# One-hot of the source rows in a GNN kernel: compared with a repeated tile of node numbers instead of with one number per partition

## The reference

```python
src = edge_index[0]
dst = edge_index[1]
msg = x[src] * edge_weight[:, None]
agg = jax.ops.segment_sum(msg, dst, num_segments=x.shape[0])
h = agg + x
h = jax.nn.relu(h @ W1 + b1)
return h @ W2 + b2
```

## Time and profile before

| | us |
|---|---|
| median of 3 runs | 3583.42 |
| lowest and highest of them | 3581.49, 3587.07 |
| the profiled execution | 3582.05 |
| its span | 3580.3 |
| of it `source_rows`, from its first `select` to its last `low_part` | about 481 |

### The profile page before, as it was taken

How to read it: one execution, slowest core, us unless ns; L and a number is a source line. 1 busy time by engine, 2 the same in 40 slices (tenths; PEclk the granted TensorE clock), 3 DMA queues, 4 the chain that set the end, 5 groups by cost and what they waited for, 6 DMA issues and landing times. The chain is left out here.

```text
span 3580.3 us, 48965 instructions
## 1 busy us (share of the span) xinstructions
PE 1964.5 (55%) x14483; PEld 1255.0 (35%) x14483; DVE 2622.0 (73%) x4729; ACT 879.1 (25%) x1649; POOL 2221.9 (62%) x2224
## 2 busy tenths in 40 slices
PE   2455555555555655555555555266505666657775
PEld 2122222222222222222222222166505555557773
DVE  5477777777677677677777777366789999977775
ACT  3122222222222222222222222011224555520002
POOL 0377777777777777777777777311275555555552
PEclk7787888888878787888888777589855555569998
DMA  9533233332332332332333332379708999989991
GB/s 307 147 102 92 91 103 91 97 97 91 98 96 90 98 96 90 100 93 91 103 91 95 98 91 72 119 273 339 279 5 269 304 305 306 303 328 412 414 402 46
DMA packets 219404, 601.78 MB, mean 168 GB/s; under 512 B 96175, under 2 KB 113455, under 8 KB 206615
## 3 DMA queue, kind: packets, MB, share of 16 engines
q1 hardware_dynamic: 147914, 385.44, 33.6%
q0 software_dynamic: 67488, 210.15, 15.8%
q10 hardware_dynamic: 3861, 4.33, 0.4%
HBM read 403.92 MB, written 195.84 MB: 168 GB/s over the span
## 5 line engine op out<-in xcount | busy, mean ns | idle before, releaser
L1085 POOL DMA_INDIRECT region_rows<-x_space,pos x1664 | 1628.8, 979 | 531.4 <-issue 505.7
L943 PE MATMUL ps_cnt<-ident,rest 128*128 128x128 f32 x832 | 177.8, 353 | 804.5 <-DVE rest L1027 804.5
L871 ACT CAST x_space<-ps_cnt 128x512 bf16<-128x512 f32 x208 | 121.9, 586 | 1456.0 <-PE ps_cnt L943 1456.0
L943 PEld LDWEIGHTS ps_cnt<-ident,rest 128*128 128x128 f32 x832 | 116.9, 177 | 979.6 <-issue 979.6
L1016 DVE TENSOR_REDUCE rank<-masked 128x8 f32<-128x784 f32 x208 | 323.0, 1553 | 21.4
L996 DVE COPY x_space<-edges_space 128x16 f32 (+1 forms) x208 | 39.2, 189 | 332.4 <-DMA region_rows<-x_space,pos 331.7
L1457 POOL TENSOR_TENSOR agg<-x_space,agg 128x576 f32<-128x576 f32 x131 | 179.4, 1369 | 143.2 <-ACT agg L1437 143.2
L929 PE MATMUL ps_fx<-window,x_space 128*64 128x512 bf16 x1248 | 240.8, 506 | 0.0
L1421 PE MATMUL ps_th<-tmp_space,x_space 128*128 128x64 bf16 x2646 | 143.1, 230 | 177.6 <-DVE x_space L1385 177.6
L1032 DVE TENSOR_TENSOR ps_agg<-ps_cnt,x_space 128x512 f32<-128x512 f32 x208 | 145.5, 700 | 128.8 <-ACT x_space L871 128.8
L906 PE MATMUL ps_th<-x_space,w_wf 128*128 128x512 f32 x416 | 224.8, 624 | 9.7 <-DMA x_space<-rbf 9.7
(11 more groups left out here) (247 smaller groups left out, 4544.3 us busy)
## 6 DMA issues: line engine op xcount, KB each, us to landing
tmp_space<-region_rows SPq DMA_DIRECT2D x98, 882.0 KB, 6.6
run_rows<-agg SPq DMA_DIRECT2D x98, 873.0 KB, 4.8
x_space<-key_rows SPq DMA_DIRECT2D x98, 576.0 KB, 5.8
x_space<-rbf SPq DMA_DIRECT2D x104, 512.0 KB, 3.7
tmp_space<-rel_rows SPq DMA_DIRECT2D x104, 512.0 KB, 4.0
region_rows<-x_space,pos POOLq DMA_INDIRECT x1664, 2.3
region_rows<-x_space SPq DMA_DIRECT2D x1, 14259.0 KB, 83.6
x_space<-part_rows SPq DMA_DIRECT2D x208, 48.0 KB, 2.0
```

The lines of the kernel that those rows point to most:

```text
L943: last = e.transpose(ps_cnt[:, t * P:(t + 1) * P], product[:, t * P:(t + 1) * P], ident[:, :])
L1085: e.indirect_dma_start(out=region_rows, out_offset=bass.IndirectOffsetOnAxis(ap=pos[j][:, t:t + 1], axis=0), in_=rows_f[j][:, t, :], in_of ...
```

## The change

A tile `node_rep`, 128x128 bf16, is added; in `set_up` DVE fills each of its rows with `node_1`. In `source_rows`, `select` compares the keys with this tile, repeated over the 9 tiles of the half, by a tensor-tensor instruction; the instruction before compared them with the one number per partition by a tensor-scalar instruction. Output, order and waits are the same.

```diff
@@ -163,6 +163,7 @@
         ident_b = sb("ident_b", [P, P], BF16)
+        node_rep = sb("node_rep", [P, P], BF16)
         ones = sb("ones", [P, P], BF16)
@@ -555,6 +556,7 @@
                     step(e.tensor_scalar(node_1, node_iota[:, 0:1], 1.0, None, ALU.add))
+                    step(e.tensor_copy(node_rep[:, :], node_1.broadcast_to([P, P])))
@@ -1382,8 +1384,9 @@
                             e.wait_ge(mm, n - 1)
-                        e.tensor_scalar(which[n % 2], key_bc[b % KB][:, (n % 2) * U * P:(n % 2 + 1) * U * P], node_1, None,
-                                        ALU.is_equal).then_inc(oh, 1)
+                        by_tile = lambda a: a.rearrange("p (t q) -> p t q", q=P)
+                        e.tensor_tensor(by_tile(which[n % 2]), by_tile(key_bc[b % KB][:, (n % 2) * U * P:(n % 2 + 1) * U * P]),
+                                        node_rep[:, None, :].broadcast_to([P, U, P]), ALU.is_equal).then_inc(oh, 1)
```

## The result

| | us |
|---|---|
| before, median of 4 runs | 3583.36 |
| changed kernel, median of 4 runs | 3640.78 (3638.10 to 3642.67) |
| ratio | 1.0154, 95% interval 1.0140 to 1.0168 |
| predicted | 3638, range 3618 to 3656 |
| `source_rows`, before and after | 481.1 and 533.5 |

What follows compares the result with a forecast made beforehand. DVE was taken to bound `source_rows`, held up by exclusion with POOL's subtraction. 98 regions at +0.57 us gave 56, less about half a microsecond: +55.5 on 3582.05 gave 3637.6, taken as 3638, range 3618 to 3656.

Steps and rivals of the forecast that it cites:

- The constant: In `set_up`, one 128x128 copy added to DVE's chain: 0.15 to 0.4 us, covered by DMA, so 0.
- S alone: `select` of a region's first half, without contention: tensor-tensor 752 ns instead of 0.51 us, a term of +0.24 us.
- S excludes GpSimd: In `source_rows`, the new `select` and POOL's subtraction still do not run together, both ways; first subtraction 1.65 us long.
- S': `select` of a region's other half, held up by POOL: issued at 3.74, ends at 5.54.
- The cycle: One region of `source_rows`, `multiply` to next region's `multiply`: 4.90 us grows by 0.57 to 5.47, 98 times.
- M': `multiply` of a region's other half: at 1.79 before, predicted at 2.02 after the change.
- P': POOL's subtraction for a region's other half: asked for at 3.57, begins at 3.67, ends at 4.91.
- 0.12 hidden in S': Second `select` hides 0.12 beside POOL, as `low_part` does, ending 0.63 behind; with 0.19 the cycle grows by 0.50.
- GpSimd slips in ahead of S: Rival: POOL's subtraction goes before a region's first `select`; a region 6.66 us, +172 us, 3754; chance 0.05.
- S' ahead of P': Rival: second `select` gets the ports before POOL's second subtraction; 3573 to 3583; chance 0.04 below 0.2%, 0.03 within.
- the order at 1.53 and at 3.67: In a region, first `select` precedes POOL's subtraction asked at 1.53; POOL's second precedes second `select` at 3.67.

Runs made afterwards that it cites:

- the two orders: Subtraction always under `multiply`, with `low_part` last or waiting for `select`, each in kernel before and changed kernel: ratios 1.0042 and 1.0138; 1.0006 and 1.0137.

## Why the prediction was right

- **DVE sets the stage.** It stayed busy 531.93 of 533.50 us; PE's matmuls took 1.62 us and covered nothing up.
- **The constant** cost 0.23 us in the set-up. DVE's chain ends at 73.1 there and the next stage's first work begins at 111.7, so the stores still cover it, and the kernel with the tile alone is at 1.0005.
- **S alone, +0.24.** 742 to 754 ns measured, 752 worked out from two bf16 comparisons of other lengths. The formula of the Trainium skill, page "VectorE: DVE Perf Modes", gives 756 as an estimate and is as near; it erred on the instruction that was taken out (456 against 516), and the sum by it, 12 us more, would have been worse.
- **S excludes GpSimd.** Yes, in both directions, as the rows from two other stages said: the subtraction asked for at 1.53 lasts 1.65 us for 1.24, and S' 1.80 for 0.74. The kernel with the numbers in PSUM shows the case without.
- **The cycle, +0.57.** 5.44 - 4.90 = 0.54. No step of the table above is off by more than 0.04 (M' comes at 2.00, P' is issued 1.53 after it instead of 1.55). The choice of 0.12 hidden in S', and not 0.19, was right: S' ends 0.62 behind P'. 98 x 0.54 = 53 us against 55.5 forecast and 52.4 measured for the stage.
- **The time.** That 3638 was within 3 us of 3640.8 is in part luck: the stage came out 3 us short of the forecast, and some 5 us outside it, which no term foresaw, made up for that. Between the two profiled executions 7.3 us lie outside the stage, 3.5 of them in `region_sums` and the rest mostly in `run_sums`, and this is scatter, as the kernel with the tile alone shows.
- **The rivals.** That GpSimd slips in ahead of S, or S' ahead of P', did not happen in the regular regions; the order at 1.53 and at 3.67 held with 0.20 and 0.19 us.

The same working missed afterwards, in the expectations for the two orders: the step that failed was "0.08 to begin", which I had taken from the distance between ACT's cast and GpSimd's start. From DVE's end to GpSimd's start it is 0.17, and a subtraction that already stands in line begins 0.14 before that end, so 0.31 us of each half went unused. And DMA waits belong in the sum as soon as a cycle is to fall under 4.9: the share of 0.90 had said so.

## To carry to other kernels

A mean of 980 ns for an instruction with a median of 516 is not its price: look for the two kinds, and for who runs beside the long one. Where DVE and GpSimd both work from SBUF, lay out one cycle with the exclusion in it, by the rows, before pricing an edit: here 0.24 us more in each of a region's two comparisons cost 0.54 us a region, or 0.10, or something between, depending on who was holding up whom and on whether DMA set the pace. The best place for the GpSimd operation was beside the DVE instruction that reads PSUM, and it had to be queued before the DVE instruction in front of that one let go; a wait that made it start after DVE's end gave the gain away again. And a late load cost more than its wait, as it let the other engine go first.

## What was not expected of the hardware

- From the end of a DVE instruction to the start of a GpSimd operation that waits for it by a semaphore: 0.17 us here. An operation that was already issued starts 0.14 us before DVE's end instead (1.38 long at 2902.68, 1.24 by itself). Waiting costs 0.31 us more than standing in line.
- A tensor-tensor of 1.34 us that takes one input from PSUM made a faster stage than one of 0.75 us that takes both from SBUF, 5.20 against 5.44 us a region.
- DMA reached 4.37 us a region, 340 GB/s over the stretch, only when its loads were issued early; at a share of 0.94 there was still 0.8% of the kernel's time to be had from the order in which SyncE issues.
